# Where the last sign count stands: one step sooner from 7 blocks on, with normalisation and verdict product early only from 10

## The chip, the cores and the metric

The kernel runs on one core of a Trainium2 chip. The metric is the device time of one execution in microseconds; three runs of the kernel before have a median of 3960.39 (3957.46 to 3961.6).

## The reference

One Macaron block over 2048 tokens of 1024 values: x = x + 0.5 ffn(norm(x)), x = x + attention(norm(x)), x = x + 0.5 ffn(norm(x)). The ffn is a router over 64 experts of which the 8 largest are kept, with one bias vector per expert. The attention has 32 query heads and 8 key heads of 32 values, rotary angles and a causal mask, and each query row keeps only its 205 largest scores:

```python
num_remain = max(min(Sq, MIN_REMAIN), Sq - int(Sq * MASK_OUT))
_, draft_indices = jax.lax.top_k(draft, num_remain)
...
scores = jnp.einsum('bhqd,bhkd->bhqk', qr, kr) / np.sqrt(HD).astype(np.float32) + mask
attn = jax.nn.softmax(scores, axis=-1)
out = jnp.einsum('bhqk,bhkd->bhqd', attn, v)
```

What is kept must be exact in every row, so the kernel has to find the 205th largest score of each row.

## The kernel before, in words

Three phases follow one another: a (first ffn, projections, rotation, a guess of every row's threshold), b (the attention), c (output projection and second ffn). The change is in phase b alone.

Phase b works on 128 places, a place p being a key head group (8 of them, 4 query heads each) and a tile of 128 query rows (16 of them). A tile with index i has i + 1 blocks of 128 keys: `blocks[p]`. Groups alternate in direction: the first goes from 1 block up to 16, the second from 16 down to 1, and so on, so there are four ascending and four descending passes. `NARROW` is 8 blocks.

For each tile, four things are done per head:

- R: PE computes the raw scores into PSUM (L886 to L891), and DVE moves them to SBUF as `sc` (evacuate, L1158).
- The search for the threshold. ACT counts, by a Sign activation with a sum over the row (L1019), how many scores are above a threshold. Count 0 uses the guess of phase a, count 1 the threshold that GpSimd (POOL) makes of count 0 (`first_update`), count 2 the one made of both (`second_update`, L1079 to L1090). Before count 2, DVE subtracts the second threshold from the scores (difference, L1170).
- From count 2, DVE takes the direction to go (directions, L1174), the 8 scores nearest to the threshold (nearest, L1183 and L1185) and picks the one of the right rank (choose, L1190 to L1199). The result has a verdict for each row, `bad`; PE multiplies it with ones (flags, L957), so that each partition has the sum, and DVE reads that (read_flag, L1203); a rare search by bits follows where a row failed. DVE then writes the additive mask `mk` for each head (L1299).
- T: PE computes the scores transposed, block of keys by block of keys, with the mask added (weights, L905 to L911); ACT takes the exponential (L1028); PE multiplies it with the values (L939), three blocks behind. M (L922 on PE, L1035 on ACT) puts the maxima of the rows into the query operand; it has a number among the T units and uses one of the same two PSUM banks, so that a unit on PE waits for the exponential or the copy two units back (`pe.wait_ge(sm["ex"], n - 1)`). At the end ACT copies the sum out (oT, L1043), PE turns it back (turn_back, L949) and DVE divides by the row's weight sum (normalise, L1305 and L1308), and SyncE stores it.

All of it is in a pipeline over steps j from -2 to 129, whose order is written out by hand for each engine, and each engine does its list in order. In step j:

- PE has the T units of tile j - 1, with M of tile j put in two before the last. Between them, at fractions of their number (`R_AT`, `NEXT_R_AT`), come R of heads 1 to 3 of tile j + 2 and head 0 of tile j + 3; turn_back of tile j - 2 follows the fifth T unit (or the last, if there are fewer); and the flag product of tile j stands at `FLAG_AT`, which is 1.0, behind the last unit, or at `EARLY_FLAG_AT`, 0.87. Where a tile's turned output is not yet normalised, the flag product waits for that (`norm`).
- ACT (`scalar_steps`) has the exponentials of tile j - 1 and M of tile j, and between them count 1 of tile j + 1 and count 0 of tile j + 2. Count 1 of a tile of up to 8 blocks stands ahead of all exponentials. Count 2 of tile j stands at the very head of step j; for a tile where `ahead` is true it stands one step sooner, among the last exponentials of step j - 1 (`TAIL` is 0.92 of the list).
- DVE evacuates head 0 of tile j + 2, takes the directions of tile j, then for each head the nearest scores of tile j and the evacuation of the next head of tile j + 2; then choose (tile j), difference (tile j + 1, four heads), normalise (tile j - 2), and the four masks of tile j with the flag read between the first and the second. Where `early_out` is true, normalise stands ahead of the fourth head's nearest scores instead, and the flag read between the second mask and the third. The step ends with a memset (L1341) that releases PE's T units of tile j in step j + 1.
- POOL has the selectors of tile j (from its count 2), the second update of tile j + 1, the split of the maxima, and the first update of tile j + 2. SyncE stores tile j - 2 once it is normalised and then loads the queries of tile j + 4.

Before the change, `ahead(p)` holds for ascending tiles from 10 blocks on and for descending ones from 9, and `early_out(j)` holds in every step j from 2 on in which `ahead(j + 1)` does.

Of the kernel before, what the change touches and what calls it, by code (L numbers as in the profile page):

```python
# [666 lines left out]
F8 = mybir.dt.float8e4  # L667
FLAG_BITS = 0x44000000
NARROW = TILES // 2
R_AT = (0.06, 0.25, 0.42)  # L670
FLAG_AT, NEXT_R_AT = 1.0, 0.75
TAIL, EARLY_FLAG_AT = 0.92, 0.87


def phase_b(nc, b, dram):
# [3 lines left out]
    blocks = [i + 1 for i in tile_of]  # L679
# [6 lines left out]
    def here(p):  # L686
        return 0 <= p < N

    def searching(p):
        return here(p) and searched[p]  # L690
# [17 lines left out]


    def ahead(p):  # L710
        return searching(p) and blocks[p] > NARROW and here(p - 2) and blocks[p - 2] >= NARROW

    def early_out(j):
        return here(j - 2) and ahead(j + 1)

    def counts(p, k):
        return [("S", p, k, h) for h in range(REP)] if searching(p) else []

    def scalar_steps(j):
        first = [] if ahead(j) else counts(j, 2)  # L720
        rest = []
        if searching(j + 1) and blocks[j + 1] <= NARROW:
            first += counts(j + 1, 1)
# [26 lines left out]
    def spread(events, n):  # L750

        at = [[] for _ in range(n + 1)]
        for f, e in events:
            at[math.ceil(f * n) if e[0] == "F" else int(f * n)].append(e)
        return at

    with ExitStack() as ctx:
# [58 lines left out]
        with nc.Block() as block:  # L816
# [52 lines left out]
            def _(pe):  # L869
# [45 lines left out]
                def maxima(p):  # L915

                    n = unit_no["M", p, 0]
                    pe.wait_ge(sm["mf"], p + 1)
                    if n >= 2:
                        pe.wait_ge(sm["ex"], n - 1)  # L920
                    for h in range(REP):
                        last = nc.tensor.matmul(psum[0:ONES_AT + PARTS_OF_MAX, 4 + n % 2, h * P:(h + 1) * P],  # L922
                                                mm[:, p % 2, h, :], b.eye16_minus[:, :], start=True, stop=True)
                    last.then_inc(sm["st"], 1)
# [17 lines left out]
                def turn_back(p):  # L942
                    pe.wait_ge(sm["ot"], p + 1)
                    if p:
                        pe.wait_ge(sm["norm"], p)
                    if chosen[min(p + 2, N)]:
                        pe.wait_ge(sm["flg"], chosen[min(p + 2, N)])
                    for h in range(REP):
                        last = nc.tensor.transpose(psum[:, 7, h * VP:(h + 1) * VP], oT[:, h * P:(h + 1) * P],  # L949
                                                   b.eye[0:VP, 0:VP])  # L950
                    last.then_inc(sm["otr"], 1)

                def flags(p):
                    if p >= 2:
                        pe.wait_ge(sm["norm"], p - 1)
                    pe.wait_ge(sm["bad"], chosen[p + 1])
                    nc.tensor.matmul(psum[:, 7, FLAGS:FLAGS + REP], b.ones16[:, :], bad[:, p % 2, :],  # L957
                                     start=True, stop=True).then_inc(sm["flagged"], 1)
# [3 lines left out]
                for j in range(-2, N + 2):  # L962
                    todo = units[j]
                    events = []
                    if here(j + 2):
                        events += [(f, ("R", j + 2, h + 1)) for h, f in enumerate(R_AT)]
                    if searching(j):
                        events.append((EARLY_FLAG_AT if ahead(j + 1) else FLAG_AT, ("F", j, 0)))
                    if here(j + 3):
                        events.append((NEXT_R_AT, ("R", j + 3, 0)))  # L970
                    at = spread(events, len(todo))
                    seen, back = 0, not here(j - 2)
                    held = None
                    for n in range(len(todo) + 1):
                        for kind, p, h in at[n]:
                            if kind == "R":
                                scores(p, h)
                            elif back:
                                flags(p)
                            else:  # L980
                                held = p
                        if n == len(todo):
                            break
                        kind, p, kb = todo[n]
                        if kind == "M":
                            maxima(p)
                            continue
                        weights(p, kb)
                        seen += 1
                        values(blocks_before[p] + kb - LAG)  # L990
                        if seen == min(LAG, blocks[p]):
                            values(blocks_before[p] - 1)
                        if not back and seen == min(LAG + 2, blocks[p]):
                            turn_back(j - 2)
                            back = True
                            if held is not None:
                                flags(held)
                    if j == N:
                        values(blocks_before[N] - 1)
                    if j == N + 1:  # L1000
                        turn_back(N - 1)
# [135 lines left out]
            def _(dve):  # L1137
# [174 lines left out]
                for j in range(-2, N + 2):  # L1312
                    if here(j + 2):
                        evacuate(j + 2, 0)
                    if searching(j):
                        directions(j)
                    for h in range(REP):
                        if h + 1 == REP and early_out(j):
                            normalise(j - 2)
                        if searching(j):  # L1320
                            nearest(j, h)
                        if here(j + 2) and h + 1 < REP:
                            evacuate(j + 2, h + 1)
                    if here(j + 2) and chunks[j + 2] == 2:
                        larger(j + 2)
                    if searching(j):
                        choose(j)
                    if searching(j + 1):
                        for h in range(REP):
                            difference(j + 1, h)  # L1330
                    if here(j - 2) and not early_out(j):
                        normalise(j - 2)
                    for h in range(REP):
                        if searching(j) and h == (2 if ahead(j + 1) else 1):
                            read_flag(j)
                        if here(j):
                            masks(j, h)
                    if searching(j):
                        fall_back(j)
                    if here(j):  # L1340
                        v.memset(fb[:, 7:8], 0.0).then_inc(sm["go"], 1)  # L1341
# [51 lines left out]
```

## Time and profile before

| | us |
|---|---|
| median of 3 runs | 3960.39 |
| the profiled execution, its own time | 3956.24 |
| its span in the trace | 3954.5 |
| PE busy in the span | 3221.4 |
| DVE busy in the span | 3179.6 |
| ACT busy in the span | 2664.7 |
| POOL busy in the span | 1420.4 |

The trace has the instructions of each engine with their start and duration in one execution. The idle time ahead of an instruction is given with what ended it. Phase b takes the span from about 590 to 3582 us. In the first ascending pass steps 5 to 9 lie at 649 to 768 us (tiles j of 6 to 10 blocks), in the first descending pass steps 23 to 25 lie at 1210 to 1274 us (tiles j of 9 to 7 blocks).

### The profile page before, as it was taken

The numbers are of one execution on the slowest core, as the hardware profiler recorded it, in microseconds if no ns is written. First come the engines' busy times: TensorE is split into PE (matmuls) and PEld (weight loads), VectorE is DVE, ScalarE is ACT, GpSimd is POOL, SyncE is SP. The second block draws the span as 40 slices with busy tenths as digits, with TensorE's granted clock in tenths as the row PEclk, the third lists the DMA queues.
The fourth block names the chain that finished last, engine by engine and source line by source line (L and its number), as shares of the span: only waits on it lengthen the run. The fifth ranks groups of instructions, "written<-read, shape, count | busy, mean of one in ns | idle before, by whom it ended". The sixth has DMA issues, their size and how long they took to land. (4 is left out here: it accounts for less than half of the span.)

```text
span 3954.5 us, 54267 instructions
## 1 busy us (share of the span) xinstructions
PE 3221.4 (81%) x15864; PEld 1498.5 (38%) x15864; DVE 3179.6 (80%) x6410; ACT 2664.7 (67%) x4577; POOL 1420.4 (36%) x3980
## 2 busy tenths in 40 slices
PE   6999957888598778887886678898777889887997
PEld 3444423333243333333433333343333334333444
DVE  4777759899898798998986899998698999882333
ACT  1222228898598688987886799898688988881111
POOL 1222215343244543443454343444444444350000
PEclk9999977999799889999997899999989999998998
DMA  3111121000010110000101000010110000002221
GB/s 121 67 69 67 67 69 24 11 10 10 6 23 16 26 31 11 10 10 7 25 20 35 13 13 10 9 24 13 25 31 11 13 8 10 13 17 99 80 80 48
DMA packets 221896, 123.85 MB, mean 31 GB/s; under 512 B 188196, under 2 KB 206884, under 8 KB 221476
## 3 DMA queue, kind: packets, MB, share of 16 engines
q1 hardware_dynamic: 221476, 119.36, 10.7%
q8 instruction: 128, 2.10, 0.2%
q14 instruction: 292, 2.39, 0.2%
HBM read 76.28 MB, written 42.99 MB: 30 GB/s over the span
## 5 line engine op out<-in xcount | busy, mean ns | idle before, releaser
L939 PE MATMUL banks<-pT,v_sb 128*65 128x512 f32 x2176 | 1148.9, 611 | 70.9 <-ACT oT L1043 69.5
L1028 ACT ACTIVATE pT<-banks 128x512 f32<-128x512 f32 x1088 | 635.7, 592 | 340.4 <-PE banks L911 335.4
L1158 DVE TENSOR_SCALAR_CACHE_REDUCE sc<-banks 128x1024 f32<-128x1024 f32 (+7 forms) x768 | 674.6, 904 | 73.5 <-PE banks L888 45.6
L886 PE MATMUL banks<-k_sb,q_sb 128*128 128x512 bf16 (+3 forms) x1280 | 475.9, 372 | 258.5 <-DVE sc L1158 222.0
L1185 DVE MAX8 near<-keys 128x8 f32<-128x256 f32 (+14 forms) x480 | 653.4, 1361 | 16.5
L1019 ACT ACTIVATE junk<-sc,tiny 128x256 fp8e4<-128x256 f32 (+14 forms) x480 | 598.9, 1250 | 37.2 <-DVE sc L1170 35.8
L1019 ACT ACTIVATE junk<-sc,t_all 128x256 fp8e4<-128x256 f32 (+14 forms) x480 | 600.4, 1251 | 33.2 <-DVE sc L1158 32.1
L905 PE MATMUL banks<-q_sb,k_sb 128*128 128x512 bf16 x1088 | 430.1, 395 | 214.5 <-ACT pT L1028 97.0
L1019 ACT ACTIVATE junk<-sc,tt 128x256 fp8e4<-128x256 f32 (+14 forms) x480 | 597.8, 1248 | 4.2 <-POOL tt L1069 4.2
L888 PE MATMUL banks<-k_sb,q_sb 96*128 96x512 bf16 (+3 forms) x1280 | 463.9, 373 | 0.0
L911 PEld LDWEIGHTS banks<-eye,mk 128*128 128x128 bf16 x4352 | 347.0, 100 | 280.4 <-issue 35.6
L911 PE MATMUL banks<-eye,mk 128*128 128x128 bf16 x4352 | 434.1, 223 | 0.0
L907 PE MATMUL banks<-q_sb,k_sb 99*128 99x512 bf16 x1088 | 428.8, 394 | 0.0
L1183 DVE TENSOR_SCALAR keys<-sc,flip 128x256 int32<-128x256 int32 (+14 forms) x480 | 393.5, 820 | 4.5 <-DVE flip L1176 0.3
L1170 DVE TENSOR_SCALAR sc<-sc,tt 128x256 f32<-128x256 f32 (+14 forms) x480 | 360.2, 814 | 19.4 <-POOL tt L1090 19.4
L1299 DVE TENSOR_SCALAR mk<-sc,dk 128x256 bf16<-128x256 f32 (+14 forms) x480 | 370.3, 814 | 0.0
L376 PE MATMUL banks<-wqkv,a_xT 128*128 128x512 f32 x768 | 352.4, 603 | 13.5 <-DVE gs L552 12.3
L886 PEld LDWEIGHTS banks<-k_sb,q_sb 128*128 128x128 bf16 x1280 | 131.4, 103 | 527.5 <-DVE sc L1158 308.9
L1066 POOL TENSOR_SCALAR dd<-sgn,tab 128x4 f32<-128x4 f32 x120 | 95.5, 795 | 542.1 <-ACT junk L1019 542.0
L1079 POOL TENSOR_SCALAR pw_b<-sgn,tab 128x4 f32<-128x4 f32 x120 | 55.7, 465 | 642.2 <-ACT junk L1019 635.3
L905 PEld LDWEIGHTS banks<-q_sb,k_sb 128*128 128x128 bf16 x1088 | 109.5, 101 | 465.7 <-ACT pT L1028 160.9
L939 PEld LDWEIGHTS banks<-pT,v_sb 128*65 128x65 f32 x2176 | 220.6, 142 | 88.0 <-issue 76.6
(230 smaller groups left out, 4394.6 us busy)
## 6 DMA issues: line engine op xcount, KB each, us to landing
q_sb<-scratch_qk SPq DMA_DIRECT2D x896, 32.0 KB, 1.9
scratch_qk<-parts SPq DMA_DIRECT2D x16, 960.0 KB, 3.7
a_x<-in_x SPq DMA_DIRECT2D x16, 512.0 KB, 4.4
scratch_x<-a_x SPq DMA_DIRECT2D x16, 512.0 KB, 3.0
scratch_attn<-o_sb SPq DMA_DIRECT2D x128, 64.0 KB, 1.6
c_xn<-scratch_attn SPq DMA_DIRECT2D x16, 512.0 KB, 3.7
c_x<-scratch_x SPq DMA_DIRECT2D x16, 512.0 KB, 4.6
out<-c_x SPq DMA_DIRECT2D x16, 512.0 KB, 2.6
```

The lines of the kernel that those rows point to most:

```text
L886: nc.tensor.matmul(r_slot(n)[:, j:j + wj], q_sb[:, p % QS, 0, h, :], k_sb[:, group[p] % 2, 0, col:col + wj], start=True, stop=False)
L888: last = nc.tensor.matmul(r_slot(n)[:, j:j + wj], q_sb[0:K1, p % QS, 1, h, :], k_sb[0:K1, group[p] % 2, 1, col:col + wj], start=False, sto ...
L905: nc.tensor.matmul(psum[:, bank, :], k_sb[:, group[p] % 2, 0, cols], q_sb[:, p % QS, 0, :, :].rearrange("p h n -> p (h n)"), start=True, s ...
L907: nc.tensor.matmul(psum[:, bank, :], k_sb[0:ONES_AT + PARTS_OF_MAX, group[p] % 2, 1, cols], q_sb[0:ONES_AT + PARTS_OF_MAX, p % QS, 1, :, : ...
L911: last = nc.tensor.matmul(psum[:, bank, h * P:(h + 1) * P], mk[:, p % 2, h, cols], b.eye16[:, :], start=False, stop=(h == REP - 1))
L939: nc.tensor.matmul(psum[0:VP, 6, :], v_sb[:, group[p] % 2, kb, :], pT[:, n % PTS, :], start=(kb == 0), stop=(kb == blocks[p] - 1)).then_in ...
L1019: nc.scalar.activation(junk[:, n % 2, 0:w], s, ACT.Sign, bias=bias, scale=scale, accum_out=into, saturate=False)\
L1028: nc.scalar.activation(pT[:, tn % PTS, :], psum[:, 4 + n % 2, :], ACT.Exp, scale=SCALE)\
L1158: v.tensor_scalar(sc[:, p % SCS, h, c * CHUNK:c * CHUNK + w], r_slot(n)[:, 0:w], 0.0, None, ALU.add, ALU.max, accum_out=mx[:, p % 4, c, h: ...
L1183: link(v.tensor_scalar(z.bitcast(I32), sc[:, p % SCS, h, 0:width[p]].bitcast(I32), 2, flip[:, h:h + 1], ALU.logical_shift_right, ALU.bitwi ...
L1185: v.max(near[:, h, :], z).then_inc(sm["key"], 1)
L1299: v.tensor_scalar(mk[:, p % 2, h, 0:width[p]], sc[:, p % SCS, h, 0:width[p]], low, MASKED, ALU.is_lt, ALU.mult).then_inc(sm["mask"], 1)
```

## The change

`SOON`, 6, takes the place of `NARROW`, 8, in `ahead`: it now also holds for ascending tiles of 7, 8 and 9 blocks and for descending ones of 8 and 7. Their count 2 goes to the step before. `early_out` gets a condition of its own, on the blocks of tile j - 1, whose exponentials the step has: 10 or more. It no longer holds in the steps of ascending tiles of 9 and 10 blocks, and it now holds in the step of descending tiles of 9. The place of the flag product on PE and of its read on DVE goes by `early_out(j)` where it went by `ahead(j + 1)`.

```diff
 NARROW = TILES // 2
+SOON = 6
...
     def ahead(p):
-        return searching(p) and blocks[p] > NARROW and here(p - 2) and blocks[p - 2] >= NARROW
+        return searching(p) and blocks[p] > SOON and here(p - 2) and blocks[p - 2] >= SOON - 1
 
     def early_out(j):
-        return here(j - 2) and ahead(j + 1)
+        return here(j - 2) and ahead(j + 1) and blocks[j - 1] > NARROW + 1
...
                     if searching(j):
-                        events.append((EARLY_FLAG_AT if ahead(j + 1) else FLAG_AT, ("F", j, 0)))
+                        events.append((EARLY_FLAG_AT if early_out(j) else FLAG_AT, ("F", j, 0)))
...
                     for h in range(REP):
-                        if searching(j) and h == (2 if ahead(j + 1) else 1):
+                        if searching(j) and h == (2 if early_out(j) else 1):
                             read_flag(j)
```

## Rows read from the trace of the kernel before

**Rows 1.** Page, part 1: engine, busy us, share of the span, instructions.

```profile
PE 3221.4 (81%) x15864; PEld 1498.5 (38%) x15864; DVE 3179.6 (80%) x6410; ACT 2664.7 (67%) x4577; POOL 1420.4 (36%) x3980
```

**Rows 2.** Timeline of DVE, steps 7 to 9: start, duration, instruction, [idle before <-releaser].

```profile
690.20 0.23 DVE L1174 TENSOR_SCALAR dirn<-sgn,tab 128x4 int32<-128x4 f32 x1 [0.78 <-ACT junk L1019]
...
704.74 3.01 DVE L1170 TENSOR_SCALAR sc<-sc,tt 128x1152 f32<-128x1152 f32 x4 [0.41 <-POOL tt L1090]
...
714.01 0.23 DVE L1174 TENSOR_SCALAR dirn<-sgn,tab 128x4 int32<-128x4 f32 x1 [1.48 <-ACT junk L1019]
...
726.92 0.18 DVE L1305 RECIPROCAL rec<-banks 128x4 f32<-128x4 f32 x1 [1.11 <-PE banks L949]
...
735.46 0.15 DVE L1203 TENSOR_SCALAR_CACHE_REDUCE heads_bad<-banks 128x4 f32<-128x4 f32 x1
...
756.39 0.18 DVE L1305 RECIPROCAL rec<-banks 128x4 f32<-128x4 f32 x1 [1.37 <-PE banks L949]
```

**Rows 3.** Timeline of DVE, steps 23 to 25.

```profile
1221.15 1.09 DVE L1158 TENSOR_SCALAR_CACHE_REDUCE sc<-banks 128x896 f32<-128x896 f32 x1 [1.00 <-PE banks L891]
...
1231.50 0.16 DVE L1203 TENSOR_SCALAR_CACHE_REDUCE heads_bad<-banks 128x4 f32<-128x4 f32 x1 [1.74 <-PE banks L957]
...
1235.76 0.23 DVE L1174 TENSOR_SCALAR dirn<-sgn,tab 128x4 int32<-128x4 f32 x1 [1.01 <-ACT junk L1019]
...
1248.78 2.47 DVE L1170 TENSOR_SCALAR sc<-sc,tt 128x896 f32<-128x896 f32 x4
...
1253.35 0.16 DVE L1203 TENSOR_SCALAR_CACHE_REDUCE heads_bad<-banks 128x4 f32<-128x4 f32 x1 [1.02 <-PE banks L957]
...
1257.17 0.23 DVE L1174 TENSOR_SCALAR dirn<-sgn,tab 128x4 int32<-128x4 f32 x1 [0.91 <-ACT junk L1019]
...
1272.30 0.16 DVE L1203 TENSOR_SCALAR_CACHE_REDUCE heads_bad<-banks 128x4 f32<-128x4 f32 x1 [0.95 <-PE banks L957]
```

**Rows 4.** Timeline of PE, the end of step 8.

```profile
731.23 0.39 PE L905 MATMUL banks<-q_sb,k_sb 128*128 128x512 bf16 x1 [1.23 <-ACT pT L1028]
...
732.76 0.17 PE L957 MATMUL banks<-bad,ones 128*128 128x4 bf16 x1
733.92 0.39 PE L905 MATMUL banks<-q_sb,k_sb 128*128 128x512 bf16 x1 [0.98 <-ACT q_sb L1035]
```

**Rows 5.** Timeline of DVE, step 5: the subtractions and the normalisation.

```profile
662.12 2.47 DVE L1170 TENSOR_SCALAR sc<-sc,tt 128x896 f32<-128x896 f32 x4
664.50 0.18 DVE L1305 RECIPROCAL rec<-banks 128x4 f32<-128x4 f32 x1
```

**Rows 6.** Timeline of ACT, step 5: M of tile 5, count 2 of tile 6.

```profile
659.01 0.59 ACT L1035 ACTIVATE q_sb<-banks 3x512 bf16<-3x512 f32 x1
...
663.32 1.03 ACT L1019 ACTIVATE junk<-sc,tiny 128x896 fp8e4<-128x896 f32 x1
```

**Rows 7.** Timeline of PE, step 5: the last scores and the turn-back.

```profile
660.83 0.38 PE L905 MATMUL banks<-q_sb,k_sb 128*128 128x512 bf16 x1
...
662.35 0.41 PE L949 MATMUL banks<-eye,oT 65*128 65x65 f32 x4
```

**Rows 8.** Timeline of ACT, steps 7 and 8: first exponential, first counts 2.

```profile
691.95 0.60 ACT L1028 ACTIVATE pT<-banks 128x512 f32<-128x512 f32 x1 [1.79 <-PE banks L911]
...
708.92 1.25 ACT L1019 ACTIVATE junk<-sc,tiny 128x1152 fp8e4<-128x1152 f32 x1
...
731.79 1.36 ACT L1019 ACTIVATE junk<-sc,tiny 128x1280 fp8e4<-128x1280 f32 x1 [0.61 <-DVE sc L1170]
```

**Rows 9.** Timeline of ACT, step 23: the copy of the finished sum.

```profile
1218.52 0.59 ACT L1043 ACTIVATE oT<-banks 65x512 f32<-65x512 f32 x1
```

**Rows 10.** Page, part 6: query loads, count, KB each, us to landing.

```profile
q_sb<-scratch_qk SPq DMA_DIRECT2D x896, 32.0 KB, 1.9
```

**Rows 11.** Windows, steps 25 and 89: length, engines' busy time, clock, DMA.

```profile
1255.51:1274.26 18.75, 15.20 (x89) 7.02 (x89) 16.44 (x39) 16.30 (x35) 9.14 (x29) 1.00 0.06 15
2751.52:2771.92 20.40, 16.86 (x89) 7.69 (x89) 16.54 (x38) 16.41 (x35) 9.12 (x29) 0.92 0.07 16
```

## The prediction

> **What bounds the kernel.** I read the page's engine table first: VectorE (DVE) is busy 80%, TensorE (PE) 81% [rows 1]. Such shares average over all stages, so the next view was each step by itself. Steps are named by j; 5 to 9 are in the first ascending pass, 23 to 25 in the first descending one, and each kind of pass comes four times. DVE paces a step: everything on it runs in order, and PE cannot start the exponentials' scores of step j+1 before DVE's last mask of step j. So a step is DVE's work plus DVE's waits, and a change that moves no work off DVE can act only through the waits. Those of the steps that the diff touches are in the timeline of DVE alone. Three kinds are to be seen there: L1174 (direction of the last sign count) waits for ScalarE (ACT), 0.78 and 1.48 us in steps 7 and 8, 1.01 and 0.91 in 24 and 25; the early normalisation L1305 waits for PE, 1.11 and 1.37 us in steps 8 and 9; the flag read L1203 waits for PE, 1.74, 1.02 and 0.95 us in steps 23 to 25 [rows 2, 3].
>
> **What the edit does to the order.** No instruction is added or removed. `ahead` becomes true for tiles of 7, 8 and 9 blocks in ascending passes and of 8 and 7 in descending ones (20 of 120 searched tiles). Their four last sign counts leave the head of ACT's list and stand among the last exponentials of the step before. `early_out` goes off in steps 8 and 9 and on in step 23, and normalise, the flag product on PE and the flag read go with it. What the edit removes is then plain: the L1174 waits above. What it adds is less visible. The first of the four counts waits for DVE's first subtraction L1170 of that step, ACT is in order, and behind it now stand the copy of the maxima (M, L1035) and the last two or three exponentials. PE's last scores of the step need M, because the two score banks alternate. And in steps 5 to 9 and 24 the flag product comes behind those last scores. So the chain is: subtraction, count, M, last scores, flag, three masks, end of the step. That PE's last scores do wait for M when a tile is `ahead` shows in step 8 today: 0.98 us for L1035, after the flag product, which stands ahead of it there [rows 4].
>
> **Step 5, tile 6 newly ahead.** The first subtraction ends at 662.12 plus a quarter of 2.47, 662.75 [rows 5]. The count of 896 takes 1.03 and M 0.59 [rows 6]: M ends at 664.45 with the hand-overs, where it now ends at 659.60. The last scores, at 660.83, move to 664.5, 3.7 later, and the turn-back L949 behind them (its end 662.76 now) to 666.45 [rows 7]. DVE wants L1305 at 664.50 [rows 5]: it waits 2.0. No L1174 wait stood in step 6 to pay for it, since that row's list starts with step 7. **+2.0**, from 1.0 if DVE reaches its subtractions earlier, to 2.5.
>
> **Step 6.** The same chain, but the turn-back stands ahead of the gated scores; count, M, scores and flag come out within 0.2 us of today's. **0**, from -0.4 to +0.6.
>
> **Step 7.** The L1174 wait (0.78) and the wait of L1170 for POOL (0.41) go. ACT starts at 691.95 as before, since that is a wait for PE, and reaches its first 1152 count at 708.92 [rows 8], 16.97 later. M (0.64 with its gaps), two exponentials (1.1) and 1.0 of its waits for PE leave that stretch, so the count starts at 706.2; the subtraction is done by 704.4 and does not decide. Count 1.25, M 0.6: the last scores start at 708.1. From the scores of one unit to the flag product is 731.23 to 732.76, 1.53 [rows 4], and the read follows some 0.25 behind: 709.85. Today it stands at 704.74 + 3.01 + 0.4 (normalise) + 0.7 (one mask), 708.8 [rows 2]. **+1.1**, from -0.8 (both waits simply gone) to 2.
>
> **Step 8.** The wait of 1.48 and the early normalisation with its 1.11 go, DVE is 2.6 early, and then the flag: M comes 0.61 earlier (its count waited that long for the subtraction [rows 8]), so the last scores move from 733.92 to 733.3 [rows 4], the flag to 734.85, the read to 735.1 against 735.46 [rows 2]. But three masks follow it instead of two, 0.75 more. **+0.4**, from -2.2 to 1.
>
> **Step 9.** The 1.37 goes; the product at the end is gated as in step 8 and takes some back. **-1.0**, from -1.6 to 0.
>
> **Step 23.** It turns early. One more first count (1.03, of that width [rows 6]) now stands ahead of the oT copy at 1218.52 [rows 9]. PE's value product waits for that copy, the next tile's scores are behind the product, and L1158, which already waits 1.00 for them, waits 2.0. The turn-back, 1.0 later too, then meets a normalisation that wants it sooner: some 0.75 more, and 0.43 for the normalisation itself. So the subtractions come 2.2 later, the first done at 1228.8. Count, exponential, count, exponential (about 1.13 and 0.55 each, between the rows of 896 and 1152) bring 1232.15, one unit and the flag 1233.95 for the read against 1231.50 [rows 3]; two masks remain instead of three. **+1.7**, from -1.7 to 2.5.
>
> **Step 24.** The L1174 wait goes (1.01), half of it is found again at L1158 (scores behind the oT copy), so the subtraction ends at 1248.78 + 0.68 - 0.55 = 1248.9. Two counts, two exponentials: 1252.2; then two units of PE, 3.05: flag 1255.25, read 1255.5 against 1253.35 [rows 3]. **+2.1**, from -2 (the waits of [rows 3] gone) to 3; with the full 1.78 of its two early waits it would be +0.9.
>
> **Step 25.** Its tile is ahead, the next is not, so nothing new stands at its end. Four counts of 896, 4.1 us [rows 6], leave the head of ACT's list, PE gets its first exponentials that much sooner, and both waits go, 0.91 and 0.95. **-1.85**, from -2.1 to -0.9.
>
> SyncE's stores follow the normalisation and its query loads follow the stores. In step 9 they slip by some 5 us; a load lands in 1.9 us [rows 10] and is read most of a step later, so it is hidden; bare it would cost that slip once per ascending pass.
>
> **The sum.** Ascending 2.0 + 0 + 1.1 + 0.4 - 1.0 = 2.5; descending 1.7 + 2.1 - 1.85 = 1.95; four of each, 17.8, say 18 us. The profiled execution took 3956.24 (span 3954.5 and 1.7 around it) and becomes 3974. The runs shown have a median of 3960.39, 4.15 above it: 3978.
>
> **Rivals.** *A, the waits just go.* If the flag arrives before DVE's first mask is over, as in early steps today, all the DVE waits named are gain: 0.78 + 0.41 + 1.48 + 1.11 + 1.37 ascending, 1.74 + 1.01 + 1.02 + 0.91 + 0.95 descending, 10.8, times four is 43: 3917. For it: in step 8 the read after an early product waits for nothing. Against it: that product stands ahead of the gated scores, and behind them in the new order. It decides for A if the count's subtraction is done 2 us or more earlier than I find. Of the Trainium skill, Perfetto Trace Analysis, "Identifying the Most-Contended Engine" and "Optimization Strategy", say that the engine of highest occupancy is to be looked at (matmul busy time left aside) and its gaps made to end sooner; by that rule the result would be A's. The rows agree on the engine and show, in step 5, a new gap that it does not count.
>
> *B, even.* The price in 5, 23 and 24 is half of mine (2.9 a pair less), the gains as they stand: 18 - 12 = 6 more, 3966, within what can be told.
>
> *C, the clock.* PE waits 2 to 4 us at new places. Step 25 ran at clock 1.00 in 18.75 us; the same step of the third descending pass at 0.92 in 20.40 [rows 11]. If each new wait in steps 5, 23 and 24 brings that 1.65, 12 of them add 20: 3998. TensorE: Matmul & The Clock Gate, Part 1 of the Trainium skill, calls the slow level of 1.2 GHz the default that activity releases. The two windows agree that a step like these can meet it and also that it need not; by the rule alone C would be the forecast.
>
> *D, no effect:* ACT reaches the moved counts no sooner than today; the order of its list excludes it for steps 24 and 25.
>
> **How the numbers follow.** Forecast 0.52, C 0.08, A or a part of it 0.25, B 0.14, D 0.01. The forecast's own range is 3966 to 3992 (its terms off by some 0.7 us a step). Of A the half with small gains is inside a range from 3936; above, C is cut at its middle, 3998. What a measurement of this kernel tells from no change is 0.2%, 8 us. Slower 0.60 (forecast and C), same 0.14, faster 0.26.
>
> **What would show it.** Right: L1174's waits in steps 7, 8, 24 and 25 gone; L1305 in step 5 waiting about 2 us for L949; L1203 waiting 2 us or more for L957 in step 24; L905 waiting longer for L1035 in total. Wrong: L1203 without a wait in 24 and 7, or step 23 shorter than 24.2 us.

## The result: 0.9% slower, over twice the predicted amount

The changed kernel took 4001.97 us (median of 4 runs, 3991.24 to 4006.56) against 3960.99 for the kernel before beside it: ratio 1.0092, 95% interval 1.0075 to 1.0109. On another chip it was 3998.38 (6 runs) against 3967.51: 1.0075 [1.0058, 1.0091]. Forecast was 3978, range 3936 to 3998. The direction was right, the time lies above the range.

The profiled execution has a span of 3989.5 us (own time 3991.24) against 3954.5. The page's engine row, to be held against [rows 1]:

```profile
PE 3244.9 (81%) x15864; PEld 1504.2 (38%) x15864; DVE 3180.7 (80%) x6410; ACT 2664.1 (67%) x4577; POOL 1411.2 (35%) x3980
```

The same instructions in the same numbers. DVE's busy time rose by 1.1 us, PE's by 23.5: products of the same shape ran longer. The 35 us between the spans are waits of DVE, no work. (The medians lie 41 apart: the profiled execution was the fastest of its four.) One of the 8 executions of the descending kernel below took 4133.17 us at a granted clock of 0.823 instead of 0.934 to 0.938; it is left out of its figures.

Cut into steps (a step ends with DVE's memset of its last flag column), the difference of the two profiles is, in us, summed over the four passes of each kind; the third column is a second profile of the changed kernel, on the other chip (span 4005.6):

| step | predicted | first profile | second profile |
|---|---|---|---|
| 5 | +8.0 | +10.8 | +15.5 |
| 6 | 0 | +3.5 | +3.3 |
| 7 | +4.4 | +3.5 | +3.5 |
| 8 | +1.6 | -2.1 | -2.0 |
| 9 | -4.0 | -0.1 | +0.2 |
| 23 | +6.8 | +9.5 | +8.4 |
| 24 | +8.4 | +10.7 | +13.2 |
| 25 | -7.4 | -9.2 | -9.2 |
| sum | +17.8 | +26.7 | +33.0 |
| all other steps | 0 | +10.6 | +17.0 |
| before and behind them | 0 | -2.3 | +1.2 |

So there are two gaps to explain: 9 to 15 us in the touched steps, and 11 to 17 in steps that the diff does not touch.

**What the new waits look like.** Lines are one higher than before from the new constant on. DVE in step 5, first pass (start, duration, instruction, [idle before <-releaser]):

```profile
661.77 2.47 DVE L1171 TENSOR_SCALAR sc<-sc,tt 128x896 f32<-128x896 f32 x4
666.33 0.18 DVE L1306 RECIPROCAL rec<-banks 128x4 f32<-128x4 f32 x1 [2.09 <-PE banks L950]
```

The normalisation that waited for nothing [rows 5] waits 2.09; 2.0 had been forecast. PE in the same step:

```profile
664.35 0.39 PE L906 MATMUL banks<-q_sb,k_sb 128*128 128x512 bf16 x1 [2.62 <-ACT q_sb L1036]
...
665.88 0.41 PE L950 MATMUL banks<-eye,oT 65*128 65x65 f32 x4
```

The last scores wait 2.62 us for M and the turn-back stands behind them; in [rows 7] the scores waited for nothing. That is the forecast chain, link by link. The place near the end of a step where PE waits for ACT is called the gate below. DVE in steps 7 to 9:

```profile
692.20 0.23 DVE L1175 TENSOR_SCALAR dirn<-sgn,tab 128x4 int32<-128x4 f32 x1
...
712.50 0.16 DVE L1204 TENSOR_SCALAR_CACHE_REDUCE heads_bad<-banks 128x4 f32<-128x4 f32 x1 [1.27 <-PE banks L958]
...
716.21 0.31 DVE L1175 TENSOR_SCALAR dirn<-sgn,tab 128x4 int32<-128x4 f32 x1
...
737.81 0.16 DVE L1204 TENSOR_SCALAR_CACHE_REDUCE heads_bad<-banks 128x4 f32<-128x4 f32 x1 [1.61 <-PE banks L958]
...
767.32 0.16 DVE L1204 TENSOR_SCALAR_CACHE_REDUCE heads_bad<-banks 128x4 f32<-128x4 f32 x1 [0.88 <-PE banks L958]
```

Held against [rows 2]: the direction's waits of 0.78 and 1.48 us are gone, and the flag read, which waited for nothing in step 8, waits in all three steps. DVE in steps 23 to 25:

```profile
1225.35 1.09 DVE L1159 TENSOR_SCALAR_CACHE_REDUCE sc<-banks 128x896 f32<-128x896 f32 x1 [2.02 <-PE banks L892]
...
1227.12 0.18 DVE L1306 RECIPROCAL rec<-banks 128x4 f32<-128x4 f32 x1 [0.67 <-PE banks L950]
...
1237.85 0.16 DVE L1204 TENSOR_SCALAR_CACHE_REDUCE heads_bad<-banks 128x4 f32<-128x4 f32 x1 [2.64 <-PE banks L958]
...
1260.91 0.16 DVE L1204 TENSOR_SCALAR_CACHE_REDUCE heads_bad<-banks 128x4 f32<-128x4 f32 x1 [3.70 <-PE banks L958]
...
1277.84 0.15 DVE L1204 TENSOR_SCALAR_CACHE_REDUCE heads_bad<-banks 128x4 f32<-128x4 f32 x1
```

Against [rows 3] the flag wait grows from 1.74 to 2.64 and from 1.02 to 3.70 and vanishes only in step 25. PE in step 24:

```profile
1256.21 0.40 PE L923 MATMUL banks<-eye_minus,mm 128*99 128x128 bf16 x4 [1.31 <-ACT pT L1029]
1257.63 0.39 PE L906 MATMUL banks<-q_sb,k_sb 128*128 128x512 bf16 x1 [1.02 <-ACT pT L1029]
```

So in the descending steps PE waits at the gate for the exponentials (pT) that stand behind the early counts in ACT's list, and not for the copy of the maxima as in step 5. Over the whole trace the direction's waits for ACT fell from 42.0 us (45 of them) to 26.9 (31), the flag's waits for PE rose from 42.2 (35) to 71.4 (43), and PE's waits for the copy of the maxima from 105.9 (121) to 132.5 (137). The first trade is a loss by itself: 15.1 us won, 29.2 lost.

**What the clock adds.** PE at the end of step 23:

```profile
1233.72 0.40 PE L923 MATMUL banks<-eye_minus,mm 128*99 128x128 bf16 x4 [1.36 <-ACT pT L1029]
1235.25 0.39 PE L906 MATMUL banks<-q_sb,k_sb 128*128 128x512 bf16 x1 [1.13 <-ACT pT L1029]
...
1235.92 1.86 PE L940 MATMUL banks<-pT,v_sb 128*65 128x512 f32 x2
1237.57 0.21 PE L958 MATMUL banks<-bad,ones 128*128 128x4 bf16 x1
```

Behind two waits that stand close together the pair of value products takes 1.86 us; in step 5 and elsewhere at full clock it takes 1.02. The flag product behind it is later by the same 0.8. Two such waits need not bring the lower level: in step 24 of the same pass, above, the clock stays at 1.00. Windows of the kernel before, steps 24 and 26 to 31 (window, length, busy time of PE, PEld, DVE, ACT and POOL with their counts, granted clock, DMA share, GB/s):

```profile
1233.87:1255.51 21.64, 17.35 (x101) 8.12 (x101) 18.39 (x38) 18.19 (x36) 8.25 (x29) 1.00 0.06 14
1274.26:1347.82 73.56, 58.23 (x343) 27.74 (x343) 57.18 (x198) 52.94 (x139) 36.24 (x127) 0.95 0.10 23
```

and of the changed kernel, steps 5, 23, 24, 24 of the second pass, and 26 to 31:

```profile
649.10:669.03 19.93, 13.33 (x66) 5.78 (x66) 17.14 (x38) 17.62 (x34) 7.78 (x30) 0.92 0.07 18
1212.84:1239.48 26.64, 20.59 (x109) 9.15 (x107) 20.35 (x39) 21.21 (x40) 9.08 (x30) 0.94 0.05 12
1239.48:1263.09 23.61, 18.76 (x108) 8.73 (x106) 18.37 (x39) 19.57 (x39) 9.65 (x31) 1.00 0.09 21
2002.02:2027.10 25.08, 19.87 (x107) 8.99 (x104) 18.34 (x39) 20.69 (x42) 10.98 (x37) 0.93 0.09 21
1280.21:1356.58 76.37, 62.31 (x343) 28.99 (x343) 57.30 (x197) 52.60 (x138) 36.72 (x127) 0.89 0.10 23
```

Step 24 costs 23.61 us where the clock stays at 1.00 and 25.08 where it is 0.93: the forecast's +2.1 and rival C's addition, both, in different passes. The flag wait shows the addition by itself. It is 3.70 us in the two passes at clock 1.00 and 5.38 in the two with a stretch at the lower level ahead of it:

```profile
2024.91 0.16 DVE L1204 TENSOR_SCALAR_CACHE_REDUCE heads_bad<-banks 128x4 f32<-128x4 f32 x1 [5.38 <-PE banks L958]
```

Steps 26 to 31, whose code is untouched, go from clock 0.95 to 0.89 and from 73.56 to 76.37 us in this pass. In the steps together, time at the lower of the two levels (1.2 GHz) rose from 376.9 us to 411.0, and to 440.8 in the second profile.

### The profile page after: what moved, and what is told of

It reads as the page before. It is cut to its first block and busy times, and to the rows that moved or that the text cites. A ratio compares the mean times of both kernels' runs of the same rounds, so it can differ in the third digit from the quotient of the medians.

```text
span 3989.5 us, 54267 instructions
## 1 busy us (share of the span) xinstructions
PE 3244.9 (81%) x15864; PEld 1504.2 (38%) x15864; DVE 3180.7 (80%) x6410; ACT 2664.1 (67%) x4577; POOL 1411.2 (35%) x3980
## 3 DMA queue, kind: packets, MB, share of 16 engines
q1 hardware_dynamic: 221476, 119.36, 10.6%
## 5 line engine op out<-in xcount | busy, mean ns | idle before, releaser
L1159 DVE TENSOR_SCALAR_CACHE_REDUCE sc<-banks 128x1024 f32<-128x1024 f32 (+7 forms) x768 | 674.5, 904 | 87.0 <-PE banks L889 55.6
```

Of the source, the lines that this page charges most:

```text
L1159: v.tensor_scalar(sc[:, p % SCS, h, c * CHUNK:c * CHUNK + w], r_slot(n)[:, 0:w], 0.0, None, ALU.add, ALU.max, accum_out=mx[:, p % 4, c, h: ...
```

## The experiments

Theory (S in the expectations): PE's gate prices the change (the early counts hold up M and the exponentials ahead of it, these the last scores, these the flag), and the clock adds to it (K). Rivals: the price sits in the new places of the normalisation and the flag; or the clock alone is the price; or ascending and descending steps affect each other. Diffs are against the changed kernel, or against the kernel before where so marked.

**1 and 2. The same kernels again.** A second profile of the changed kernel, and one of the kernel before.

> The changed kernel once more, to have a second profile and more times of it. Theory S (the steps' own prices): the touched steps cost 18 to 27 us against before, whatever else happens, and the rest of the 41 us is chance that differs from run to run: the touched steps repeat within 2 us, the total scatters by 10 us or more. Theory K (slow clock): beyond the touched steps' price the extra time is half of the additional time that TensorE spends at its lower level; span minus half the slow time stands 11 to 19 us above before in every profile, and the median stays about 40 us above before.

> The kernel before once more, for a second profile of it, since its first one is among its fastest executions. Theory S: the steps that the edit touches take the same times as in the first profile within 1 us a step, and what differs lies in other steps. Theory K: the difference in span is half of the difference in slow time.

The first is the third column above, 1.0075. By the expectation's measure, span less half of the time at the lower level in the steps, the two profiles stand 17.9 and 19.2 us above the first profile of before, close to the forecast's 17.8; but the touched steps did not repeat within the 2 us expected (26.7 and 33.0). The measure is no general price of the clock: by it kernel 10 below, whose time is that of the kernel before, would stand 84 us above.

The second: 3962.86, span 3961.1, touched steps +0.9 us and other steps +4.4 against the first profile of before, with 9.4 us more at the lower clock. Single touched steps differ by up to 1.7 us in one pass, where the stretch at the lower level falls elsewhere. So a difference of some 4 us in the untouched steps can be scatter; 11 and 17 are more than that.

**3 and 4. The two kinds of pass apart.** Each keeps the change in one kind of pass.

```
     def ahead(p):
-        return searching(p) and blocks[p] > SOON and here(p - 2) and blocks[p - 2] >= SOON - 1
+        edge = SOON if p // TILES % 2 == 0 else NARROW      # == 1: descending alone
+        return searching(p) and blocks[p] > edge and here(p - 2) and blocks[p - 2] >= (edge - 1 if edge == SOON else edge)
     def early_out(j):
-        return here(j - 2) and ahead(j + 1) and blocks[j - 1] > NARROW + 1
+        return here(j - 2) and ahead(j + 1) and (blocks[j - 1] > NARROW + 1 or j // TILES % 2 == 1)      # == 0: descending alone
```

> The edit in ascending passes alone (tiles of 7, 8 and 9 blocks ahead, early places off in steps 8 and 9). Theory S, by my sum: +10 us, steps 5 to 9 as in the changed kernel (+2.2, +0.9, +0.9, -0.6, -0.7 as its profile shows, 11 a kernel), and this and the descending half add up to the whole, 41. Theory K: +11 from the steps plus a slow-clock surcharge of its own that need not be half of the whole's; span minus half the slow time 8 to 12 above before.

> The edit in descending passes alone (tiles of 8 and 7 blocks ahead, early places on in step 23). Theory S, by my sum: +8 us; by the steps of the changed kernel's profile (+2.4, +2.7, -2.3) +11. Theory K: the waits of steps 23 and 24 are where slow stretches appeared that were not there before, so this half carries most of the surcharge in the touched steps: slow time in steps 23 and 24 about 14 and 7 us in all where before had none.

Ascending alone 3983.97, 1.005 [1.0036, 1.0063]; descending alone 3978.91, 1.0032 [1.002, 1.0043]. The excesses of 0.50% and 0.32% add up to 0.82%, the whole change to 0.75%. Steps 5 to 9 of the ascending kernel give +15.2, steps 23 to 25 of the descending one +12.5 (9.3, 12.4, -9.2). The parts are nearly independent. Step 23 of the ascending kernel, where nothing is changed, took 1.27 us more in one pass, with the clock lower there; so does the second profile of before (1.37).

**5. The counts alone.** The new `ahead`, but normalisation and flag keep the places that the old rule gives them.

```
     def early_out(j):
-        return here(j - 2) and ahead(j + 1) and blocks[j - 1] > NARROW + 1
+        p = j + 1
+        return here(j - 2) and searching(p) and blocks[p] > NARROW and here(p - 2) and blocks[p - 2] >= NARROW
```

> Only the sign counts move; normalise, flag product and flag read stay where they were before. Steps 8 and 9 keep the early places, step 23 the late ones. By the chain of the prediction: step 5 +2.0, step 7 +1.1, step 8 -0.7 (its L1174 wait goes, the early product is not gated), step 9 0, step 23 +3.0 (its late product is gated by M behind three counts), 24 +2.1, 25 -1.85: 22 us in all, 5 more than the whole edit by the same chain. Rival: if the late places in steps 8 and 9 and the early ones in 23 are what costs, this kernel is nearer to before than to the changed one, under +10.

3995.89, 1.0074 [1.006, 1.0088], as the whole change. Step 23 +11.5 (2.9 a pass), step 8 -3.0, step 24 +11.8. The moved places of normalisation and flag are worth about nothing in sum; that rival is out.

**6. The early counts behind M.** The changed kernel, with the first newly early count right behind M in ACT's list and the others after it. M and the exponentials ahead of it no longer wait for these counts, everything else stays.

```
-        return steps + rest[done:]
+        out = steps + rest[done:]
+        if ahead(j + 1) and not (blocks[j + 1] > NARROW and blocks[j - 1] >= NARROW):
+            early = counts(j + 1, 2)
+            out = [s for s in out if s not in early]
+            m = out.index(("M", j, 0, 0))
+            head, tail = out[:m + 1], out[m + 1:]
+            at = [n for n, s in enumerate(tail) if s[0] == "T"]
+            out = head + early[:1] + tail[:at[-1]] + early[1:3] + tail[at[-1]:] + early[3:]
+        return out
```

> The changed kernel with one difference in ACT's order: the four early counts of the newly ahead tiles stand behind M (one between M and the exponential after it, two before the last exponential, one at the end) instead of up to three ahead of M. If the chain count, M, last scores, flag is what the edit costs (theory S), the prices go: step 5 0, step 7 -0.3, step 8 -0.7, step 9 about 0, step 23 about +0.2, step 24 -0.6, step 25 -1.5 against before, 12 us under before in all, give or take 8, and no slow stretch stands at the end of steps 23 and 24. Rival: the price comes from the first counts that stand closer together ahead of the oT copy, and from the places of normalise and flag, which are as in the changed kernel: then +20 or more stays.

3967.21, 1.0008 [0.9999, 1.0018]: the loss is gone. ACT and DVE in its step 5:

```profile
665.36 0.59 ACT L1044 ACTIVATE q_sb<-banks 3x512 bf16<-3x512 f32 x1
667.39 1.04 ACT L1028 ACTIVATE junk<-sc,tiny 128x896 fp8e4<-128x896 f32 x1 [1.44 <-DVE sc L1179]
```

```profile
666.62 2.47 DVE L1179 TENSOR_SCALAR sc<-sc,tt 128x896 f32<-128x896 f32 x4
669.00 0.17 DVE L1314 RECIPROCAL rec<-banks 128x4 f32<-128x4 f32 x1
```

ACT still waits 1.44 us for the subtraction, but M (L1044 here) is ahead of that wait, and the normalisation finds its operand at once, as before the change. Its windows of steps 5, 23 and 24:

```profile
653.92:671.71 17.79, 13.14 (x66) 5.85 (x66) 17.09 (x38) 16.06 (x32) 7.41 (x29) 0.88 0.09 20
1214.33:1238.24 23.91, 19.97 (x115) 9.14 (x112) 20.26 (x38) 19.34 (x36) 8.42 (x29) 1.00 0.07 17
1238.24:1261.15 22.91, 17.35 (x101) 8.11 (x101) 18.40 (x38) 19.27 (x39) 7.32 (x29) 1.00 0.08 18
```

In this pass step 5 is back at its 17.8 us, step 23 at 23.9, the clock in 23 and 24 is 1.00, and the flag wait of step 24 is back at 1.02. In sum the touched steps give -0.3 us instead of +26.7. But the gain of 12 us that was expected does not come out either: step 24 keeps +6.0 over four passes and step 25 only -5.5. In step 24 the direction now waits 1.38 us for the counts behind M (1.01 before) and the evacuation 1.67 (0.77 before). The counts fit neither ahead of M nor behind it without a price.

**7. The clock held in steps 23 and 24.** The changed kernel with 16 small products ahead of M's product and of the second-last scores; they write into a corner that nobody reads.

```
+                        if j // TILES % 2 and 9 >= blocks[j] >= 8 and here(j) and (kind == "M" or kb == blocks[p] - 2):
+                            for _ in range(16):
+                                nc.tensor.matmul(psum[96:128, 6, 0:128], b.eye16[:, 96:128], b.eye16[:, :], start=True, stop=True)
```

> The changed kernel with 16 small products on TensorE, written to a part of PSUM that nothing reads, ahead of M and ahead of the second last scores in steps 23 and 24, where it waits 1.0 to 1.5 us for ACT. They take about 0.9 us of each wait and no work away. If the slow stretches at the end of these steps (13.6 and 6.8 us in the four passes) come from TensorE's waiting there and cost time, they go or shrink and steps 23 and 24 fall to 26.0 and 23.3 us in every pass: 7 to 10 us less than the changed kernel. If the gate alone sets these steps, nothing changes, or it gets slower by what the products add.

3989.26, 1.0057 [1.0045, 1.0069]. Windows of steps 23, 24, and 24 of the second pass:

```profile
1218.10:1243.91 25.81, 21.71 (x143) 10.64 (x141) 20.35 (x38) 20.82 (x40) 8.45 (x29) 1.00 0.05 13
1243.91:1267.81 23.90, 20.28 (x139) 10.27 (x136) 18.29 (x39) 19.86 (x40) 9.31 (x31) 1.00 0.09 20
2002.38:2026.50 24.12, 20.28 (x139) 10.28 (x136) 18.29 (x38) 19.85 (x40) 9.27 (x31) 1.00 0.09 21
```

The clock is 1.00 in all three, and steps 23 and 24 cost +5.8 and +9.2 instead of +9.5 and +10.7 (or +8.4 and +13.2). Per pass that is +1.6 (three passes, +0.9 in the last) and +2.3: the forecast's 1.7 and 2.1. The flag wait of step 24 is 3.70 in all four passes,

```profile
2024.32 0.16 DVE L1207 TENSOR_SCALAR_CACHE_REDUCE heads_bad<-banks 128x4 f32<-128x4 f32 x1 [3.70 <-PE banks L958]
```

and that of step 23 is 1.81, where the changed kernel has 2.64 and 3.28 in the passes with a stretch at the lower level ahead of it. The added products cost a little themselves: step 24 of the changed kernel takes 23.61 and 23.06 us in its two passes at clock 1.00, against 23.9 to 24.1 here. So the sum's terms were about the price at full clock, and the clock put 5 to 7 us on top in these steps. Most of the price stays without it: the rival "the clock alone" is out.

**8 and 9. One count instead of four** (both against the kernel before). A single count goes early, ahead of M in steps 23 and 24; kernel 8 also puts one behind M in step 6.

```
+    def one_soon(p):
+        return searching(p) and blocks[p] in (7, 8) and p // TILES % 2 == 1     # kernel 8: also 8 blocks, ascending
...
-        first = [] if ahead(j) else counts(j, 2)
+        first = [] if ahead(j) else counts(j, 2)[1 if one_soon(j) else 0:]
...
-        return steps + rest[done:]
+        out = steps + rest[done:]
+        if one_soon(j + 1):
+            m = out.index(("M", j, 0, 0))
+            out.insert(m if (j + 1) // TILES % 2 else m + 1, ("S", j + 1, 2, 0))
+        return out
```

> The kernel before, with one count of the four moved one step sooner, and only where ACT has a gap for it after DVE's first subtraction: ahead of M in steps 23 and 24 (gaps of 1.20 and 1.10 us there) and behind M in step 6 (gap of 0.93). Nothing else moves. Theory S: the count fits into the gap, M comes at most 0.4 later, which the last scores do not notice, and the L1174 waits of 1.01, 0.91 and 0.78 us go: 10.8 us less than before. Rival: any count ahead of M costs what it saves, because M and the flag come later: within 3 us of before.

> The one early count in descending passes alone (ahead of M in steps 23 and 24), without the one in step 6, which moved nothing in the run before. Steps 24 and 25 lose 1.1 and 0.75 us in each of four passes as they did there, 7.5 to 9 us. Theory S: the time falls by that, 0.2%, unless slow stretches elsewhere take it back. Rival: what is gained in these two steps is refound later in the pass, and the time stays within 3 us of before.

Kernel 8: 3965.56, 0.9998 [0.9987, 1.0009]; kernel 9: 3962.11, 0.9995 [0.9986, 1.0003]. Windows of kernel 9, steps 24, 25, and 26 to 31:

```profile
1238.38:1258.89 20.51, 17.35 (x101) 8.11 (x101) 18.29 (x39) 17.80 (x36) 8.39 (x28) 1.00 0.06 15
1258.89:1276.90 18.01, 15.20 (x89) 7.03 (x89) 16.44 (x39) 15.56 (x33) 9.37 (x31) 1.00 0.07 16
1276.90:1354.46 77.56, 62.35 (x343) 29.08 (x343) 57.28 (x198) 53.02 (x139) 35.82 (x127) 0.89 0.09 22
```

Steps 24 and 25 gain 1.13 and 0.74 us (in all passes together 8.9 against the first profile of before, 8.7 against the second) and step 23 loses nothing: the subtraction of the first quarter is done in time for one count. Then steps 26 to 31 take 77.56 us at clock 0.89 instead of 73.56 at 0.95. Over all passes the descending steps of 1 to 5 blocks lose 4.6 us against the first profile, with 13.7 us more at the lower clock, and 6.8 with 17.1 against the second. So the gain is real, and half of it or more is given back where no instruction was changed. In step 6, kernel 8's count moved nothing in step 7 (-0.02 us a pass).

**10, 11, 12. One count, and PE kept at work** (against the kernel before). Kernel 10 has small products alone: 24 at the start of ascending steps, 16 ahead of the first scores of descending ones. Kernel 11 has these and the one early count of kernel 9. Kernel 12 is kernel 11 without the products in descending steps of 10 blocks or more.

```
+                    def busy(n):
+                        for _ in range(n):
+                            nc.tensor.matmul(psum[96:128, 6, 0:128], b.eye16[:, 96:128], b.eye16[:, :], start=True, stop=True)
+                    up = j // TILES % 2 == 0
+                    if here(j) and up:
+                        busy(24)
...
+                        if kb == 0 and here(j) and not up:      # kernel 12: and blocks[j] < 10
+                            busy(16)
```

> The kernel before with small products on TensorE in the waits at the start of each step of the attention: 24 ahead of the first scores in ascending passes (it waits 3.2 to 3.7 us for DVE there) and 16 ahead of the exponentials' scores in descending ones (1.7 to 1.8 us, for the masks). They write to a part of PSUM that nothing reads. Theory K: slow time in the attention falls from about 380 us to under half, and the time by some 10 to 30 us, since steps with a slow stretch took 0.7 to 1.7 us more. Theory S: DVE's work bounds a step, the waits of DVE for PE at the start of a step are 0.4 to 1 us in few steps: under 8 us.

> Both together: one early count in descending passes and the small products at the start of each step. If both act as expected and do not meet, the gains add: 15 to 35 us under before. If the slow stretches are what took the early count's gain back, it is more than the products alone give by 8 us; if not, it is the same as the products alone within 3 us.

> One early count in descending passes and the small products at the start of each step, but not in descending steps of 10 blocks and more: there TensorE has no time to spare, and in the run before steps of 10 to 14 blocks took 0.7 to 1.1 us longer each, which is what 16 products take, some 18 us in all. Without them those steps go back to their times and the rest stays: 16 to 20 us under the kernel with both, 3930 us, 0.9% under before. Rival: the products in these steps also kept the clock up for the steps that follow, and part of the 18 comes back as slow time: 5 to 10 us under the kernel with both.

Kernel 10: 3962.83, 0.9994 [0.9986, 1.0003], though time at the lower level in the steps fell from 376.9 us to 235.5. Kernel 11: 3947.71, 0.9956 [0.9943, 0.9968]. Kernel 12: 3926.33 (3920.93 to 3928.98) against 3966.39, **0.9897 [0.988, 0.9913]**, faster than both kernels of this case.

Kernel 10's gain is eaten in descending steps of 10 to 14 blocks, 16.4 us over the passes against the second profile of before. There PE has no time to spare: in such a step of kernel 11 no idle time stands ahead of the products,

```profile
1192.97 1.07 PE L983 MATMUL banks<-eye 128*32 128x128 bf16 x16
```

They take 1.07 us, and most of those steps grew by 0.7 to 1.1. Kernel 10 also spoils step 24 (clock 0.93 there):

```profile
1240.93:1263.97 23.04, 19.84 (x117) 9.45 (x117) 18.42 (x39) 18.31 (x36) 8.25 (x29) 0.93 0.06 14
```

Kernel 12, steps 24, 25, and 26 to 31:

```profile
1231.94:1252.45 20.51, 18.35 (x117) 9.00 (x117) 18.29 (x38) 17.79 (x36) 8.39 (x28) 1.00 0.06 15
1252.45:1270.46 18.01, 16.20 (x105) 7.92 (x105) 16.44 (x39) 15.56 (x33) 9.37 (x31) 1.00 0.07 16
1270.46:1343.42 72.96, 62.32 (x441) 32.57 (x442) 56.89 (x197) 52.91 (x139) 36.26 (x127) 0.98 0.10 24
```

All of the early count's gain is there, and the steps behind keep 0.98. Against the second profile of before, its descending steps of 6 to 9 blocks give -11.6 us, those of 1 to 5 blocks -3.8, those of 10 and more -2.5, the ascending ones -21.1; together 39, and the spans differ by 38.1. By one profile of each, each half alone lost what the other half holds: kernel 9 the clock in the narrow steps (+6.8, here -3.8), kernel 10 the clock in step 24 (1.4 us in three passes, here -1.1 in all four). Kernels 10 and 11, on one chip, differ by 15 us, which is what the one count is worth where the products stand. The products of kernel 12 without the count were not run.

## Why the prediction was too small

**The mechanism was right.** The waits that were to go are gone; L1306 in step 5 waits 2.09 (2.0 forecast), L1159 in step 23 2.02 (2.0), L1306 there 0.67 (0.75), L1204 in step 24 more than 2, and PE's waits for the copy of the maxima rose by 26.6 us. Experiment 6 shows that the gate is the price: with M ahead of the counts the touched steps cost nothing in sum. Rival A, all waits as gain, is refuted with it. The Trainium skill (Perfetto Trace Analysis, "Optimization Strategy") says to find the gaps on the engine in question and to make what ends them start sooner. Applied to L1174 alone this ended 15.1 us of waits here and made 29.2 of others: what is started sooner stands in front of something else. B is refuted by the size, D by the trace. (In the forecast's chances D's 0.01 is counted as faster, though D forecasts no change.)

**The step that failed is "The sum".** It adds eight terms, read in the first pass, and has none for a change of the clock, while rival C, the clock, stood beside it as an alternative of 0.08. The runs show that the two come together. Experiment 7 has the terms of steps 23 and 24 at clock 1.00 (but for the last pass of step 23), +1.4 and +2.3 a pass on average, where 1.7 and 2.1 were forecast. The clock then adds 5 to 7 us in steps 23 and 24. In step 5 L1306 waits 2.09 in three passes of the first profile, which is the forecast's +2.0. Where a stretch at the lower level stands right ahead, it waits longer, 2.65 in the fourth pass and 3.75 in two passes of the second profile:

```profile
675.19 0.18 DVE L1306 RECIPROCAL rec<-banks 128x4 f32<-128x4 f32 x1 [3.75 <-PE banks L950]
```

The passes in which step 5 cost 3 to 5 us have this, or 0.6 to 1.3 us of L1175 waiting for ACT at the step's start, or both; that second wait stands in single passes of the kernel before, too (1.25 in its second profile). This was a matter of reading [rows 11] as a probability and not as a term: the two windows had shown that a step like these can run at 0.92, and then takes 1.65 us more.

**The untouched steps had no term at all.** +10.6 and +17.0 us. Descending steps of 1 to 5 blocks have 17.1 us more at the lower level in both profiles of the changed kernel and in both kernels with one early count, against the second profile of before, and cost 6.2 to 7.4 us more. Against the first profile it is 13.7 us more and 4.0 to 5.2. The ascending kernel, whose descending passes are those of before, has none of this (0.0 against the second profile), the descending kernel has all of it (17.1 and 6.5 us): this part goes with the edit in the descending passes. In these kernels the steps ahead end at other times than before; which step falls to the lower level in a given pass, and why, is not shown. Since the second profile of before already differs by 4.4 us from the first, I can't say how much of the rest belongs to the change.

**Smaller terms.** Step 6: 0 forecast, +0.9 measured. PE there:

```profile
686.40 0.41 PE L950 MATMUL banks<-eye,oT 65*128 65x65 f32 x4
687.06 0.39 PE L906 MATMUL banks<-q_sb,k_sb 128*128 128x512 bf16 x1 [0.25 <-ACT q_sb L1036]
```

The last scores now meet the gate by 0.25, and the lower-clock stretch of this step has moved to a later place in it, so the scores for DVE come later too (the flag read waits 0.78, before 0.39). Step 8: +0.4 forecast, -0.5 measured, with less of the lower clock in it (3.4 us instead of 6.5 in the first pass; in the third, with 4.7 instead of 5.4, the step is as long as before). Step 9: -1.0 forecast, 0 measured. Three passes give -0.7, -0.6 and -0.2, the third +1.4. That step in the third pass, before,

```profile
2277.34:2304.59 27.25, 20.43 (x111) 9.02 (x111) 25.07 (x47) 23.85 (x38) 10.33 (x29) 1.00 0.06 13
```

and after:

```profile
2298.25:2326.93 28.68, 21.95 (x111) 9.61 (x111) 25.18 (x47) 23.80 (x36) 10.86 (x29) 0.94 0.05 12
```

In this pass it ran at full clock before, with 0.42 us of L1305's wait to give back and not 1.37, and lost that clock. The term was read from the first pass, and I took four equal passes; this was to be seen in the trace before. Step 25 gained 2.3 a pass instead of 1.85, the third pass again apart (-3.5, where before it had run at 0.92 [rows 11]).

In figures, the first profile's touched sum exceeds the forecast by 8.9: step 5 +2.8, step 6 +3.5, step 7 -0.9, step 8 -3.7, step 9 +3.9, step 23 +2.7, step 24 +2.3, step 25 -1.8. The other steps add 10.6, the stretches around them take 2.3.

## What to carry to other kernels

An item moved forward in an in-order list is priced by what stands behind it at its new place, not by the wait that it ends at its old one: follow the list from there to the next engine's gate, and move only as much as is ready in time. Here that was one count of four (20.51 us for step 24 against 21.64), and the other three cost more than the whole wait. Where a change adds waits of an engine whose clock follows its activity, put the clock into the sum as a term of its own, pass by pass, and look at the steps behind the change as well as those in it.

## What the runs showed that I had not expected

Sixteen to 24 small products of about 1 us and more in PE's idle time raise the mean granted clock of the whole kernel from 0.94 to 0.965, and combined with a move that alone gave nothing they are worth 1.0%. The clock row of the profile's page, for the kernel before:

```profile
PEclk9999977999799889999997899999989999998998
```

and the rows of the fastest kernel:

```profile
PE 3293.2 (84%) x17976; PEld 1597.0 (41%) x17976; DVE 3177.0 (81%) x6410; ACT 2662.6 (68%) x4577; POOL 1404.1 (36%) x3980
...
PEclk9999979999799999998998899999999999998998
```

PE has 2112 instructions more than in [rows 1] and 72 us more of busy time, and by the medians the kernel is 40 us shorter. TensorE: Matmul & The Clock Gate, Part 1 of the Trainium skill, calls the 1.2 GHz level the default that activity releases; these runs agree, for a kernel that is bound by another engine. A higher mean clock is not yet a gain, though: kernel 10, at 0.959, was as slow as the kernel before. Its products also stood where PE had no idle time, and without those the time fell (kernel 12 against 11).
